# Reciprocal roots of the last layer norms: seven VectorE operations each, or one power on GpSimd

## The reference, cut to what matters

```python
logits = (x @ gate_w + gate_b) / TEMP                 # two of eight experts, softmax over the two
h = gelu(einsum('bsd,edf->bsef', x, w1) + b1)
out = einsum('bse,bsed->bsd', gate_probs, einsum('bsef,efd->bsed', h, w2) + b2)
out = (out - mean(out)) / sqrt(var(out) + 1e-5) * ln_g + ln_b      # first norm ("head")
y = x + out
return (y - mean(y)) / sqrt(var(y) + 1e-5)                         # second norm ("tail")
```

## Time and profile before

| | us |
|---|---|
| median of 3 runs | 321.38 |
| lowest and highest run | 318.09, 323.15 |
| profiled execution, span from first to last instruction | 316.4 |
| PE busy | 246.8 (78%) |
| DVE busy | 176.4 (56%) |
| ACT busy | 180.0 (57%) |
| POOL busy | 174.8 (55%) |

### The profile page before, as it was taken

One profiled execution on the slowest core, in us unless ns is written; L12 is line 12 of the kernel. 1 busy time (PEld: TensorE's weight loads), 2 busy tenths in 40 slices (PEclk: granted clock), 3 DMA queues, 4 the chain that ended last, 5 costly groups with the idle time before them and its releaser, 6 DMA issues.

```text
span 316.4 us, 7585 instructions
## 1 busy us (share of the span) xinstructions
PE 246.8 (78%) x1867; PEld 222.5 (70%) x1868; DVE 176.4 (56%) x961; ACT 180.0 (57%) x536; POOL 174.8 (55%) x296
## 2 busy tenths in 40 slices
PE   2998977959968774799798999999999999940000
PEld 2576766757746664799597999999999999940000
DVE  0135767755687482252482243256459779786763
ACT  3257746646456465474475665465555698667044
POOL 8100065768686688847886656656665675661000
PEclk9999999989979768599798999999999999995555
DMA  5896111212213144122213668777599668212404
GB/s 136 240 328 198 35 58 45 68 39 72 76 44 101 43 111 119 61 64 64 59 45 101 188 193 233 236 219 210 182 313 324 182 206 278 82 55 83 134 0 133
DMA packets 44770, 42.38 MB, mean 134 GB/s; under 512 B 5408, under 2 KB 33488, under 8 KB 44736
## 3 DMA queue, kind: packets, MB, share of 16 engines
q1 hardware_dynamic: 40416, 33.10, 35.9%
q0 software_dynamic: 4320, 8.92, 8.1%
HBM read 27.89 MB, written 12.01 MB: 126 GB/s over the span
## 4 chain that ended last, share of the span: by engine, by line
PE 61%; DVE 16%; issue 9%; ACT 6%; DVEq 3%; another core or an unknown queue 1%; DMA 1%; SPq 0%; ACTq 0%
PE bank L532 19%; PE bank L543 17%; PE bank L400 6%; PE bank L427 4%; PE bank L386 3%; DVE sum_stats L1040 3%; PE bank L515 2%; PE bank L391 2%; DVEq L1026 2%; PE bank L415 2%; PE bank L448 2%; DVE pair L1032 2%; ACT probs L617 1%; DVE sum_moments L1043 1%; PE bank L440 1%
## 5 line engine op out<-in xcount | busy, mean ns | idle before, releaser
L680 ACT ACTIVATE h<-bank,b_cols 128x128 f32<-128x128 f32 x284 | 80.3, 375 | 61.6 <-PE bank L532 40.2
L1164 POOL DMA_INDIRECT returned<-x,slot_back x71 | 71.5, 1008 | 50.6 <-DVE x L1002 32.0
L532 PE MATMUL bank<-slot_xT,w_now 128*128 128x128 f32 x568 | 81.3, 287 | 3.0 <-issue 2.2
L543 PE MATMUL bank<-w_all,h 128*128 x568 | 82.2, 288 | 1.5 <-issue 1.3
L532 PEld LDWEIGHTS bank<-slot_xT,w_now 128*128 128x128 f32 x568 | 74.6, 204 | 2.9 <-issue 2.8
L543 PEld LDWEIGHTS bank<-w_all,h 128*128 128x128 f32 x568 | 71.5, 196 | 3.6 <-issue 2.6
L1157 POOL DMA_INDIRECT slots<-rows,slot_of x64 | 61.8, 966 | 17.8 <-issue 11.1
L1150 POOL MEMSET pause_out<- 1x200 f32 x131 | 33.4, 255 | 41.4 <-DVE rows L874 40.9
L785 DVE CAST slot_back<-slot_x 128x1 uint32<-128x1 f32 x71 | 10.5, 147 | 67.3 <-PE bank L532 44.0
L690 ACT ACTIVATE pair<-pair,sum_shift,sum_rstd 128x128 f32<-128x128 f32 x62 | 25.5, 493 | 17.4 <-DVE sum_shift L1015 17.4
L427 PEld LDWEIGHTS bank<-v,probsT 128*128 128x128 f32 x160 | 21.4, 201 | 11.5 <-issue 7.7
(11 more groups left out here) (153 smaller groups left out, 322.1 us busy)
## 6 DMA issues: line engine op xcount, KB each, us to landing
w_now<-in_L_ffn_w_dram SPq DMA_DIRECT2D x47, 256.0 KB
slot_x<-slots SPq DMA_DIRECT2D x71, 65.0 KB
w_all<-in_L_ffn_w_dram SPq DMA_DIRECT2D x16, 256.0 KB, 5.0
pair<-returned SPq DMA_DIRECT2D x16, 256.0 KB, 2.7
x<-n_L_attn_embeddings_dram SPq DMA_DIRECT2D x8, 256.0 KB, 4.4
rows<-rows SPq DMA_DIRECT2D x8, 256.0 KB, 2.9
returned<-x,slot_back POOLq DMA_INDIRECT x71
slots<-rows,slot_of POOLq DMA_INDIRECT x64
```

What stands on the lines that cost most here:

```text
L532: m = nc.tensor.matmul(o, w1_now[:, s, cols], slot_xT[:, s % RING, :], start=True, stop=True)
L543: m = nc.tensor.matmul(o, h[:, s % RING, c * P:(c + 1) * P], w2_c, start=False, stop=(c == FC - 1))
L680: m = nc.scalar.activation(h[:, s % RING, cols], bank_[:, cols], ACT.Gelu, bias=b1_cols[:, c:][:, bass.ds(first, 1)])
L1164: g_.indirect_dma_start(returned, bass.IndirectOffsetOnAxis(ap=slot_back[:, j:j + 1], axis=0), y[:, j % Y_RING, :], None).then_inc(y_retur ...
```

## The change

In `set_rstd` third 0 now writes only var + eps and raises `var_ready`; third 1 does nothing; third 2 waits for `power_ready` and then forms `sum_shift`. The seven operations of `rsqrt_step` and their drains are gone from DVE, for all six (set, norm) pairs. POOL raises `sum_var` to the power -0.5, given as a tensor of constants `minus_half`, which one more memset fills at the start. POOL has its own order: the first two powers stand behind `give_back(51)` and `give_back(63)`, the third, of (1, head), behind `give_back(68)` and so ahead of `give_back(69)` and `give_back(70)`, and the other three behind the last of these.

```diff
-        NCONST, FIRST_CONST = 13 + B, 4
+        NCONST, FIRST_CONST = 14 + B, 4
...
+        ROOT_AFTER = (51, 63, J - 3)
...
-            def set_rstd(n, third):
+            def set_rstd(n, tail, third):
+
                 t0, t1 = SETS[n]
-                rstd_, var_, tmp_ = sum_rstd[:, t0:t1], sum_var[:, t0:t1], sum_tmp[:, t0:t1]
                 one = "p (t a) -> p t a"
                 if third == 0:
-                    vec.tensor_scalar(var_.rearrange(one, a=1), sum_moments[:, t0:t1, 1:2], EPS, None, ALU.add)
-                    dve.drain()
-                for q in ((0, 1), (2, 3, 4), (5, 6, 7))[third]:
-                    rsqrt_step(q, rstd_, var_, tmp_)
-                    dve.drain()
-                if third == 2:
+                    vec.tensor_scalar(sum_var[:, t0:t1].rearrange(one, a=1), sum_moments[:, t0:t1, 1:2],
+                                      EPS, None, ALU.add).then_inc(var_ready, 1)
+                elif third == 2:
+                    dve.wait_ge(power_ready, 2 * n + tail + 1)
                     vec.scalar_tensor_tensor(out=sum_shift[:, t0:t1].rearrange(one, a=1), in0=sum_moments[:, t0:t1, 0:1],
...
+            g_.memset(minus_half[:], -0.5).then_inc(const_ready, 1)
...
+            def reciprocal_root(k):
+
+                t0, t1 = SETS[ORDER[k][0]]
+                pool.wait_ge(var_ready, k + 1)
+                g_.tensor_tensor(sum_rstd[:, t0:t1], sum_var[:, t0:t1], minus_half[:, t0:t1], ALU.pow).then_inc(power_ready, 1)
+
             for j in range(RETURNS_AHEAD, J):
                 give_back(j)
+                if j in ROOT_AFTER:
+                    reciprocal_root(ROOT_AFTER.index(j))
+            for k in range(len(ROOT_AFTER), len(ORDER)):
+                reciprocal_root(k)
```

More of the change, by code:

```diff
@@ L165, in moe_block @@
         sum_rstd, sum_shift = sb("sum_rstd", [P, NT]), sb("sum_shift", [P, NT])
+        minus_half = sb("minus_half", [P, NT])
         bank = [ctx.enter_context(nc.psum_tensor(f"bank{i}", [P, 512], F32)) for i in range(8)]
@@ L219, in moe_block @@
         pair_loaded = [sem(f"pair_loaded{b}") for b in range(B)]
+        var_ready, power_ready = sem("var_ready"), sem("power_ready")
         moments_ready = [sem(f"moments_ready{n}") for n in range(len(SETS))]
@@ L1027, in final_unit @@
                 if q >= units(n, tail) - 3:
-                    set_rstd(n, q - (units(n, tail) - 3))
+                    set_rstd(n, tail, q - (units(n, tail) - 3))
                 elif tail and what == 0:
```

## The result

The changed kernel takes 326.46 us in the median of 4 runs, and the kernel before, on the same chip, 322.26. The ratio is 1.0177, with a 95% interval from 1.0129 to 1.0224: about 5.7 us more (4.2 to 7.2). The two medians lie only 4.2 us apart, because they are taken over all runs, while the ratio compares runs in the undisturbed state alone. The forecast was 2.5 us less, and its range, up to 323.0, does not hold the result. The profiled execution of the changed kernel has a span of 325.3 us; its own time was 327.12, 1.8 us over the span. In the four executions of the changed kernel that have both numbers, the difference is 1.75 to 1.82. So the profile of the kernel before (316.4) belongs, in all likelihood, to the run of 318.09, the fastest of its three, and not to the median.

The account below looks back on a forecast made before the run. PE was taken to set the pace until about 281 us, DVE's chain after it, then the stores. Three roots gaining 2.4 us and (0, tail) 0.1 made 2.5 us: 321.38 to 318.9 us, range 314.8 to 323.0.

Parts of the forecast that it names:

- The power's price, taken as 1.0 us for all sizes: On POOL, each root's power p was forecast at 1.0 us for 16, 12 and 4 numbers alike; bounds 0.18 and 1.71.
- the bare roots: (1, head), (1, tail), (2, head), after PE's last matmul: each forecast to fall from 2.42 to 1.62 us, 2.4 gained in all.
- The signals: Between DVE and POOL at each root: 0.24 us to POOL and 0.04 us back.
- the covers: Power lengths hidden at the two roots in the steps: up to 1.23 us at (0, tail), 2.25 us at (0, head).
- The root of (2, tail) is worth nothing for the stores: Last root, at the end: nothing gained if faster, no cost until 1.0 us slower, because of the store stream.
- The stalls of 0.23 and 0.41 us: Excess of (1, head) and (1, tail) over 2.42 us on DVE; not counted, 0.6 us kept for the range.
- The give-backs behind the third power cost nothing: On POOL, give-backs 69 and 70 end 2.1 us later; six microseconds of cover remain for the last sequence's load.
- The first use of the power: Rival: at (0, head), the first power fetches its code, a first use of e costing e - 2.25 us; chance 0.05.
- The offset of 5.0 us between span and median: Whole kernel: the median of the runs, 321.38 us, was taken as 5.0 us above the profiled span of 316.4.
- the power about eats the gain: Rival: power of 1.4 to 2.2 us, between 1.2 us gained and 2.2 lost, about 321.3 us; chance 0.24.
- the power goes through numbers one after another: Rival: power of 3 us or more, DVE waiting in third 2; 327.7 us at p = 3.0; chance 0.11.
- The balance at p = 1.66: Power length in us at which the gain of the three bare roots equals the loss at (0, tail).

## Why the prediction was wrong

- **The power's price, taken as 1.0 us for all sizes: this step failed.** It took 2.95, 2.30 and 1.01 us for 16, 12 and 4 numbers, which fit 0.36 + 0.162 n, and the power of 8 numbers, worked out ahead as 1.66, took 1.64. I knew that no row showed a power, and took the indirect DMA as the nearest; it was right by accident for n = 4. The upper bound of 1.71 us by the longest POOL instruction was no bound, since that row is a fill and not arithmetic. The slip is the words "for 16, 12 and 4 numbers alike": an unknown cost should have had a part for each number, and the two dearest roots had four times as many numbers as the cheapest. With the measured prices the prediction's own sum gives 2 x 0.5 lost and 0.8 gained at the bare roots, 1.7 lost at (0, tail) and 0.7 at (0, head): 2.6 us slower in place of 2.5 faster.
- **The second failed step, a term that was not in the sum at all: POOL's exit**, 2.8 us. I asked who waits for POOL's work, but not when POOL itself is done. The row was there: a closing drain that ended 8.4 us behind the last give-back. The list of what is queued on POOL ought to have ended with the end of the program. For the same reason (2, tail) was put at nothing though its power, POOL's last instruction, set the end.
- **The mechanism of the sum, each root priced by DVE's wait beyond its cover, was right; three of its sizes were off, and they partly cancel.** The signals took 0.09 and 0.03 us, not 0.24 and 0.04. The roots of (1, head) and (1, tail) took 2.65 and 2.83 us before, not 2.42. And in the steps the power started right behind its give-back (0.02 us at (0, tail)) and not 0.24 us behind it, so that the covers were 1.45 and 2.47 us, not 1.23 and 2.25. With these sizes the bare roots gain 0.9, (0, tail) loses 1.5 and (0, head) 0.5, and the whole is 1.1 us slower; with the exit 3.9. The stages of the bare roots (+0.11 - 1.04) and of (0, tail) (+1.48) agree. That of (0, head), +1.49, doesn't: about 1 us of it is the scatter told of above.
- **The root of (2, tail) is worth nothing for the stores**: right. 1.45 us in the changed kernel and 2.74 with that root back on DVE made no difference to the stores' stream, which was full for the last 3.7 us in both.
- **The stalls of 0.23 and 0.41 us "may turn up elsewhere"**: partly. In the changed kernel they did not. But in the run with the last root back on DVE a stall of 0.41 us stands ahead of the last `sum_shift`, and in the two with only (0, head) on POOL the root of (1, tail) took 2.48 us while a stall of 0.40 us stands ahead of a unit behind it. (1, head) took 2.65 to 2.67 us in all six other profiles that had it on DVE.
- **The give-backs behind the third power cost nothing**: right. The last ended 5.1 us behind the start of that root's `sum_var`, where it was 1.9 before: 3.2 us later and not 2.1, as the power was longer. The last sequence's load was never waited for.
- **The first use of the power**: 0.04 us, 1.05 as the first and only one against 1.01.
- **The offset of 5.0 us between span and median** was no property of the kernel. It is 1.8 us for each run; the profiled run was the fastest of three. It did not move the difference that was forecast.
- Of the rivals, "the power about eats the gain" had p at 1.4 to 2.2, and the mean of the six powers was 2.09; "the power goes through numbers one after another" had the right mechanism, a price by the number, and p = 3 us is what the 16 numbers took. Its 327.7 us comes near the measured time by luck, since it has p = 3 for the small roots too and no exit. The balance at p = 1.66 had been worked out, and stood closer to the chosen 1.0 than the knowledge of p allowed.

## What to carry to other kernels

An operation that no row shows gets a price of two parts, a fixed one and one for each number, before it is put in for tiles of different size; and the rows that bound it must do the same kind of work. A slow operation on an idle engine is worth having where its user can go on with other work: all six made the kernel slower when DVE stood waiting for them, and three of them made it 1.8% faster than the kernel before when one was collected late and one cut so that the first consumer could start. Before work is given to an engine late in a program, look at how long that engine takes to leave it.

## What the runs showed of the hardware that was not expected

- A power of two fp32 tensors on POOL over 128 partitions took 0.36 + 0.162 n us for n numbers a partition (n = 4, 8, 12, 16: 1.01, 1.64, 2.30, 2.95), a multiplication 0.20 to 0.23 us for n = 4 to 16. The first power of a program took up to 0.04 us more than the later ones of its size.
- POOL needed 8.4 to 8.5 us from reaching the end of its program to leaving it. That was so behind an indirect DMA, a power, a multiplication, a memset, and a mere wait. It costs whatever reaches beyond the last store: 2 to 2.8 us here. Whether the 135 indirect DMAs that POOL issues earlier have a part in it was not tried.
- A power of 2.31 us on POOL beside an addition (0.69 us) and statistics (0.87 us for four) on DVE lengthened none of the three.
- From the end of a DVE instruction to the start of an arithmetic one on POOL that waited for it: 0.09 us, and 0.03 back.
